# Attention's score columns of 32 heads, packed across head boundaries into chunks of 1536

## The reference, cut to what matters

```python
qkv = (x @ Wqkv + bqkv).reshape(B, L, 3, n_heads, head_dim)     # B 2, L 2048, 16 heads of 16
scores = einsum('bqhd,bkhd->bhqk', q, k) / sqrt(head_dim)
scores = scores + slopes[h] * -abs(pos_k - pos_q)               # slope of head h: 2 ** (-h / 2)
probs = softmax(scores)
out = einsum('bhqk,bkhd->bqhd', probs, v) @ Wout + bout
x = layernorm(x + out)
x = layernorm(x + experts(x))                                   # 7 experts and a pass-through, top 2
```

## Time and profile before

| | |
|---|---|
| runs of the kernel | 1083.63, 1084.35, 1084.83 us; median 1084.35 |
| the profiled execution | 1084.32 us, span 1082.5 us |
| granted TensorE clock, mean | 0.978 |
| PE, ACT, DVE, POOL busy in the span | 95%, 75%, 41%, 28% |
| attention: first to last exponential | 115.4 to 802.3 us |

### The profile page before, as it was taken

One profiled execution on the slowest core, in us unless ns is written; L12 is line 12 of the kernel. 1 busy time (PEld: TensorE's weight loads), 2 busy tenths in 40 slices (PEclk: granted clock), 3 DMA queues, 4 the chain that ended last, 5 costly groups with the idle time before them and its releaser, 6 DMA issues. The chain is left out here.

```text
span 1082.5 us, 38401 instructions
## 1 busy us (share of the span) xinstructions
PE 1033.4 (95%) x16944; PEld 680.0 (63%) x16944; DVE 438.4 (41%) x1030; ACT 816.3 (75%) x822; POOL 304.9 (28%) x454
## 2 busy tenths in 40 slices
PE   9999899999999999999999999999998389999997
PEld 6555665566576675876655757757587246666665
DVE  5777334453342332225434624323257711111165
ACT  3564899999999999999999999999966164111252
POOL 3334122122121121112221521211240254554443
PEclk9999999999999999999999999999999579999999
DMA  5755312222221111112342132121209246544473
GB/s 188 222 186 169 110 53 80 59 62 64 61 59 58 50 46 44 49 42 74 93 116 60 46 81 52 47 57 33 83 10 286 55 118 185 123 113 112 113 277 135
DMA packets 76554, 104.74 MB, mean 97 GB/s; under 512 B 13774, under 2 KB 62556, under 8 KB 76380
## 3 DMA queue, kind: packets, MB, share of 16 engines
q1 hardware_dynamic: 65852, 87.94, 26.4%
q0 software_dynamic: 6080, 9.06, 4.1%
q10 hardware_dynamic: 4448, 5.19, 1.6%
HBM read 66.49 MB, written 31.48 MB: 91 GB/s over the span
## 5 line engine op out<-in xcount | busy, mean ns | idle before, releaser
L999 ACT ACTIVATE prob<-ps 128x1536 f32<-128x1536 f32 (+4 forms) x504 | 664.8, 1468 | 24.8 <-PE ps L955 23.4
L955 PE MATMUL ps<-q_stack,k_stack 99*32 99x128 bf16 (+19 forms) x8390 | 449.2, 304 | 9.8 <-ACT prob L999 7.9
L979 PE MATMUL ps<-prob,v_head 128*32 128x128 f32 (+7 forms) x7228 | 446.0, 339 | 0.9 <-DVE prob L1010 0.7
L955 PEld LDWEIGHTS ps<-q_stack,k_stack 123*32 123x32 bf16 (+3 forms) x8390 | 239.2, 96 | 177.1 <-ACT prob L999 106.5
L979 PEld LDWEIGHTS ps<-prob,v_head 128*32 128x32 f32 x7228 | 251.8, 110 | 66.9 <-issue 5.0
L1010 POOL TENSOR_TENSOR prob<-prob,near_bias 128x128 f32<-128x128 f32 x256 | 125.4, 494 | 530.6 <-ACT prob L999 530.3
L1010 DVE TENSOR_TENSOR prob<-prob,near_bias 128x128 f32<-128x128 f32 x256 | 83.6, 334 | 430.7 <-ACT prob L999 430.6
L1028 DVE RECIPROCAL o_rec<-o_den 128x128 f32<-128x128 f32 x128 | 113.0, 922 | 0.6
L1704 PE MATMUL ps<-xeT,w 128*128 128x512 f32 x224 | 100.3, 606 | 0.8 <-ACT xeT L1735 0.7
L1718 PE MATMUL ps<-w,hT 128*128 128x256 f32 x448 | 98.7, 382 | 0.0
L1781 ACT ACTIVATE hT<-ps 128x512 f32<-128x512 f32 x28 | 16.7, 596 | 108.5 <-PE ps L1704 108.5
(11 more groups left out here) (173 smaller groups left out, 604.7 us busy)
## 6 DMA issues: line engine op xcount, KB each, us to landing
qk_parts<-split SPq DMA_DIRECT2D x32, 384.0 KB, 3.1
w<-L_ffn_experts_inter_dram SPq DMA_DIRECT2D x7, 1024.0 KB, 6.4
w<-n_L_ffn_experts_out_dram SPq DMA_DIRECT2D x7, 1024.0 KB, 9.7
q_stack<-qk_parts SPq DMA_DIRECT2D x31, 192.0 KB
k_stack<-qk_parts SPq DMA_DIRECT2D x31, 192.0 KB
z_rows<-v SPq DMA_DIRECT2D x8, 516.0 KB, 9.3
heads<-o_out SPq DMA_DIRECT2D x128, 32.0 KB, 2.4
v<-in_L_attn_x_dram SPq DMA_DIRECT2D x8, 512.0 KB, 6.2
```

Source lines behind the costliest of these rows:

```text
L955: mm = pe.matmul(ps[k:k + keys, SLOT_BANKS * (c % 2) + bank, col:col + z - a], k_st[n % STACKS][0:rows, kb * P + k:kb * P + k + keys], q_s ...
L979: mm = pe.matmul(ps[32 * g:32 * g + 32, 6 + n % 2, column:column + width * times], vh[n % 2][:, kb, :], moving, start=g not in begun, stop ...
L999: act.activation(prob[:, c % RING, 0:at + z - a], ps[:, bank:bank + SLOT_BANKS, :].rearrange("p c n -> p (c n)")[:, 0:at + z - a], ACT.Exp ...
```

## The change

All 32 items are laid end to end as one run of columns, which is cut every 1536. `packed` fills each item's columns in behind those of the item before. To let the next item begin at a multiple of 128 columns inside a chunk, the last key block of an item may take in up to 112 more queries on its left side, in steps of 16 (`more` in `spans`). A chunk may now hold pieces of two items, so each piece carries its item's number `n`, and each wait that belongs to an item's first chunk (stack, copy of values, output bank) stands at the chunk in which the item begins. A shared chunk is scored in strips or not by its first item. `FIRST` and `LAST` come from the chunks in which an item occurs, and with them the times of the divisions, loads, copies and biases. The exponential of a shared chunk is one activation. The functions not shown change only in that a piece has `n` in front.

```diff
-def band_plan(h):
-
-    chunks, at = [[]], 0
-    for kb in range(KB):
+def spans(h, more):
+
+    return [(kb, max(0, kb * P - reach(h) - (more if kb == KB - 1 else 0)), min(L, kb * P + P + reach(h))) for kb in range(KB)]
+
+
+def fill(n, h, at, more, width=WIDTH):
+
+    chunks = [[]]
+    for kb, a, end in spans(h, more):
         k0 = kb * P
-        a, end = max(0, k0 - reach(h)), min(L, k0 + P + reach(h))
         while a < end:
-            z = min(end, a + WIDTH - at)
+            z = min(end, a + width - at)
             if k0 < z < k0 + P:
                 z = k0
             if z > a:
-                chunks[-1].append((kb, a, z, at))
+                chunks[-1].append((n, kb, a, z, at))
             at += z - a
-            if z < end or at == WIDTH:
+            if z < end or at == width:
                 chunks.append([])
                 at = 0
             a = z
-    return [c for c in chunks if c]
+    return chunks if chunks[-1] else chunks[:-1]
+
+
+def filled(chunk):
+
+    return max((at + z - a for _, _, a, z, at in chunk), default=0)
+
+
+def packed(items):
+
+    chunks = [[]]
+    for n, (b, h) in enumerate(items):
+        at = filled(chunks[-1])
+        mine = next(new for new in (fill(n, h, at, more) for more in range(0, P, 16))
+                    if n + 1 == len(items) or filled(new[-1]) % P == 0)
+        chunks = chunks[:-1] + [chunks[-1] + mine[0]] + mine[1:]
+        if filled(chunks[-1]) == WIDTH:
+            chunks.append([])
+    return [chunk for chunk in chunks if chunk]
 
 
...
-PLANS = [band_plan(h) for h in range(H)]
-CHAIN = [(n, r) for n, (b, h) in enumerate(ITEMS) for r in range(len(PLANS[h]))]
-FIRST = [CHAIN.index((n, 0)) for n in range(len(ITEMS))]
-LAST = [c - 1 for c in FIRST[1:]] + [len(CHAIN) - 1]
-
-
-def chunk_of(c):
-    n, r = CHAIN[c]
-    return PLANS[ITEMS[n][1]][r]
+CHAIN = packed(ITEMS)
+CHUNK_COUNT = len(CHAIN)
+
+
+def items_of(c):
+    return sorted({n for n, *_ in CHAIN[c]})
+
+
+USES = [[c for c in range(CHUNK_COUNT) if n in items_of(c)] for n in range(len(ITEMS))]
+FIRST, LAST = [uses[0] for uses in USES], [uses[-1] for uses in USES]
 
 
 def own_blocks(c, odd):
 
-    return [own_column(piece) for piece in chunk_of(c) if own_column(piece) is not None and piece[0] % 2 == odd]
-
-
-CHUNK_COUNT = len(CHAIN)
+    return [(ITEMS[piece[0]][1], own_column(piece)) for piece in CHAIN[c] if own_column(piece) is not None and piece[1] % 2 == odd]
+
...
 def scores_in_strips(c):
-    return ITEMS[CHAIN[c][0]][1] >= IN_STRIPS
+    return ITEMS[items_of(c)[0]][1] >= IN_STRIPS
...
         def score(c):
-            n, r = CHAIN[c]
-            if r == 0:
-                pe.wait_ge(stack_in[n % STACKS], (n // STACKS + 1) * 16 * (LOADS + 1))
+            for n in items_of(c):
+                if c == FIRST[n]:
+                    pe.wait_ge(stack_in[n % STACKS], (n // STACKS + 1) * 16 * (LOADS + 1))
             if c >= 2:
                 pe.wait_ge(expd, c - 1)
-            for piece in chunk_of(c):
-                kb = piece[0]
+            for piece in CHAIN[c]:
+                n, kb = piece[:2]
                 for rows, a, z, at in score_cuts(piece):
                     bank, col = divmod(at, CH)
                     keys = 32 if scores_in_strips(c) else P
@@ -959,27 +981,27 @@
             mm.then_inc(scored, 1)
 
         def pv(c):
-            n, r = CHAIN[c]
             pe.wait_ge(expd, c + 1)
             if OWN_DONE[0][c] > 0:
                 pe.wait_ge(diag_even, OWN_DONE[0][c])
             if OWN_DONE[1][c] > 0:
                 pe.wait_ge(diag_odd, OWN_DONE[1][c])
-            if r == 0:
-                pe.wait_ge(vh_done, n + 1)
-                if n >= 2:
-                    pe.wait_ge(o_read, n - 1)
-            begun = {g for chunk in PLANS[ITEMS[n][1]][:r] for g, *_ in value_turns(chunk)}
-            for g, kb, at, column, width, times in value_turns(chunk_of(c)):
+            begun = {(n, g) for n in items_of(c) for d in range(FIRST[n], c) for g, m, *_ in value_turns(CHAIN[d]) if m == n}
+            for n in items_of(c):
+                if c == FIRST[n]:
+                    pe.wait_ge(vh_done, n + 1)
+                    if n >= 2:
+                        pe.wait_ge(o_read, n - 1)
+            for g, n, kb, at, column, width, times in value_turns(CHAIN[c]):
...
-                               vh[n % 2][:, kb, :], moving, start=g not in begun, stop=False,
+                               vh[n % 2][:, kb, :], moving, start=(n, g) not in begun, stop=False,
                                skip_group_check=True)
-                begun.add(g)
+                begun.add((n, g))
...
         for c in range(CHUNK_COUNT):
-            n, r = CHAIN[c]
-            if r == 0:
+            for n in items_of(c):
+                if c != FIRST[n]:
+                    continue
                 b, h = ITEMS[n]
                 if n >= 2:
                     pool.wait_ge(pv_done, LAST[n - 2] + 1)
```

More of the change, by code:

```diff
@@ L101, in band_plan @@
             a = z
-    return [c for c in chunks if c]
+    return chunks if chunks[-1] else chunks[:-1]
[11 more added lines that the diff above has]
+    return [chunk for chunk in chunks if chunk]
 def own_column(piece):
-    kb, a, z, at = piece
+    n, kb, a, z, at = piece
     return at + kb * P - a if a <= kb * P < z else None
 def score_cuts(piece):
-    kb, a, z, at = piece
+    n, kb, a, z, at = piece
     k0 = kb * P
@@ L128, in value_runs @@
         column = j // GROUPS * P + s - j * P
-        if e - s == P and mine and mine[-1][3] == P:
-            mine[-1][4] += 1
+        if e - s == P and mine and mine[-1][4] == P:
+            mine[-1][5] += 1
         else:
-            mine.append([kb, at + s - a, column, e - s, 1])
+            mine.append([n, kb, at + s - a, column, e - s, 1])
     return runs
@@ L199 @@
 DIVIDE = divide_plan()
-OWN_DONE = [list(itertools.accumulate(len(own_blocks(c, odd)) for c in range(len(CHAIN)))) for odd in range(2)]
+OWN_DONE = [list(itertools.accumulate(len(own_blocks(c, odd)) for c in range(CHUNK_COUNT))) for odd in range(2)]
 def chunk_tiles(ch):
@@ L996, in banded_scalar @@
                 act.wait_ge(pv_done, c - RING + 1)
-            kb, a, z, at = chunk_of(c)[-1]
+            n, kb, a, z, at = CHAIN[c][-1]
             bank = SLOT_BANKS * (c % 2)
@@ L1003, in near_blocks @@
     def near_blocks(eng, c, odd, done):
-        h = ITEMS[CHAIN[c][0]][1]
         if own_blocks(c, odd):
             eng.wait_ge(expd, c + 1)
-        for at in own_blocks(c, odd):
+        for h, at in own_blocks(c, odd):
             here = prob[:, c % RING, at:at + P]
```

## The result

The changed kernel takes 1074.57 us in the median of four runs (1073.24 to 1075.56), the kernel before 1084.24 beside it: 9.7 us less, a ratio of 0.9908 with a 95% interval of 0.9886 to 0.9930. Two later measurements of the pair, with 1088.15 and 1085.40 us for before, give 0.9894 (0.9870 to 0.9917) and 0.9902 (0.9883 to 0.9921). The forecast was 1074.7 in a range of 1071.0 to 1079.0.

What follows compares the result with a forecast made beforehand. ScalarE was taken to bound the attention stretch at about 1.34 us a chunk, with TensorE almost as full. Terms -0.4 - 9.1 + 2.7 - 2.6 + 0.7 - 0.9 = -9.6 took 1084.3 to 1074.7 us, range 1071.0 to 1079.0.

Steps and rivals of the forecast that it cites:

- Part 1: ScalarE's exponentials: 504 to 489 chunks saves 1.0 us, 672 padding columns cost 0.56; together -0.4 us.
- Parts 2 and 3: Starts of narrow heads: fourteen gaps behind 512-column last chunks go, -9.1 us; heads 0 to 4 give 2.7 back.
- Part 3: Narrow heads 0 to 4, paced by TensorE: part of ten removed gaps returns as later waits, +2.7 us.
- Part 4: Starts of wide heads: gaps behind short last chunks shrink, TensorE's arrears of 0.29 us each stay; -2.6 us.
- Part 5: TensorE's scores: 559 more matmuls, or 140 sets of four, at most 0.005 us a set; +0.7 us.
- Part 6: Last head: x's rows load earlier, so GpSimd's late bias and the 0.79 us gap with start-up go; -0.9 us.
- Part 7: Shared chunks: waits for stack, copy of values and output bank sit elsewhere, covered by slack; cost 0.
- A: Rival, chance 0.10: narrow heads give all ten gaps of heads 0 to 4 back; -5.8 us, 1078.5 us.
- B: Rival, chance 0.04: all gaps at head edges go and none comes back; -19 us, 1065 us.
- C: Rival, chance 0.04: TensorE becomes the bound, each added set of score matmuls showing its 0.096 us load; +3.1, 1087.4 us.
- D: Rival, chance 0.03: gaps come from each head's start (stack, copy or bank wait) and reappear there; 1084.6 us.

Runs made afterwards that it cites:

- narrow-only kernel: Changed kernel, but only narrow heads may begin in the wide head's last chunk; wide heads start their own chunk: 1074.75 us, ratio 0.9924.
- doubled cuts: Kernel before, with each full-bank cut of 512 score columns made of two of 256: 1094.80 us, ratio 1.0067.
- fewer cuts: Changed kernel, but heads may begin only at multiples of 512 columns, one bank: 1073.61 us, ratio 0.9929.
- wide-only kernel: Changed kernel, but only wide heads may begin in the narrow head's last chunk; narrow heads start their own chunk: 1076.03 us, ratio 0.9941.
- later-bias version: Changed kernel, loads of x's rows still together, but GpSimd adds the last four biases four chunks later each: 1076.19 us in one run.

## Why the prediction was right, step by step

The mechanism held, and the median fell by 9.7 us where 9.6 was forecast. That it is right to 0.1 us is luck: the interval of the ratio spans 7.6 to 12.4 us, the two later pairs give 12.2 and 10.6, the stretch in the profile fell by 10.7, and three terms were off by about 2 us each, two one way and one the other.

- Part 1, columns and activations: -0.4 forecast, -0.4 in the trace.
- Parts 2 and 3, narrow heads: -9.1 + 2.7 = -6.4 forecast. All fourteen gaps went. Heads 0 to 4 fell by 4.2, heads 5 to 7 by 3.3, and the last head had one such gap, 0.6: -8.1. Part 3 was mis-sized, and miscounted: heads 0 to 4 have eight of the fourteen gaps, not ten, since head 0 follows a chunk of 1280 columns. These eight are 5.2 us with their start-ups, and 1.0 came back (as at 182.53) where I had 2.7. That figure hangs on counting shared chunks with the wide head; in the narrow-only kernel, which has no such chunks, 1.5 came back (13.2 - 9.5 = 3.7).
- Part 4, wide heads: -2.6 forecast, -4.6 in the trace (-3.6 and -4.5 in the two later profiles). Mis-sized as well: I left 0.29 us at each start as TensorE's arrears. Behind heads 5, 6 and 7 the changed kernel has no gap at all; the arrears remain behind heads 0, 1, 3 and 4. With only the wide side packed it was -2.6 by the same count. The sum of parts 2 to 4, -12.7 where I had -9.0, doesn't hang on the count.
- Part 5, cuts: +0.7 forecast, at 0.005 us a set. The doubled cuts give 0.001 outside thirteen chunks and 0.005 with them; fewer cuts gave nothing visible back. So it lies between 0.1 and 0.7, and the sum below has no term for it.
- Part 6, the bias: the wait went as forecast, and is worth 0.9 by itself. What the step missed is that with the same loads issued earlier beside the scores TensorE stands idle for 2 us: the last head has +1.3 from the two, where I had -0.9.
- Part 7: no wait of TensorE for a stack, a copy or an output bank shows in the waits of the changed kernel. The 0 holds there; the wide-only kernel has one such wait, of 1.45 us.
- Item 0 took 1.1 us more than in the profile of before, with the clock at 0.50 two microseconds later. The changed kernel's second profile has 0.5, so this isn't the change's doing.

The sum in the trace: -0.4 - 8.1 - 4.6 + 1.3 + 1.1 = -10.7, the stretch's. The gains of parts 2 to 4 were 3.7 us larger than forecast, and part 6 with item 0 took 3.3 of it back. With the 0.7 of part 5, for which this sum has no term, that makes the 1.1 us by which the stretch fell more than forecast. A is out by the narrow-only kernel, B since 17 us of excess remain in heads 0 to 7 and wide heads, where it leaves some 12, C by the doubled cuts, D by the heads that begin a chunk of their own without a gap.

## What to carry to other kernels

Where two engines pass chunks to each other through two buffers, a short chunk starves the one that drains: its work must last as long as filling the next buffer takes, so the remainder of one piece of work should share a chunk with the start of the next. What that frees is bounded by the arrears of the other engine, so measure how long that engine was idle in the gap and not only how long the gap is. And before loads are made earlier, ask what else uses the queues then.

## What the runs showed of the hardware that was not expected

- TensorE stood for 1.8 to 2.1 us behind 2 MB of loads that filled the DMA engines, in all four profiles of the changed kernel and its later-bias version; loads three chunks apart removed it in two out of two. The kernel before, with the same loads bunched, has no such stand. In ten stands of this kind, over seven kernels, the weight loads went on 1.0 to 1.5 us behind the end of a 16 KB packet of the instruction queue.
- The same eight value matmul records, of 384 columns in four column groups, took 0.79 us between scores of 128 keys and 0.67 between scores in 32-key strips.
- Activations in a queue cost 0.833 ns a column and 0.064 us each; one on an idle engine 0.17 us more than its columns (1.45 for 1536). For an activation without pointer operands the Trainium skill (ScalarE: Activation LUTs, What ACT_TABLE_LOAD costs) gives 186 ns and 0.833 a column, 93 ns less back to back: the trace agrees on the column and is 16 and 29 ns below on the rest.
- The same chunks of item 0 cost ScalarE between 0 and 1.9 us of gaps from one execution to the next. Where TensorE's granted clock stays at 1.00 it is 0.0, with 3.4 us at 0.50 it is 0.4 to 1.6, with 6.8 us 1.9. Why the clock falls in some executions and not in others, no run here says.
